# Soft MoE weights split in the cross-attention stage, and mu moved in 256 KB pieces in the routed experts

## The reference

```python
x = x + tanh(g_xattn[0]) * L0_xattn(ctx, ctx, layernorm(x), ssm_kernel, D, 8)     # long convolution
x = x + tanh(g_ffn[0])   * L0_ffn(layernorm(x), ...)      # shared expert + 8 routed experts, top 2
x = x + tanh(g_xattn[1]) * L1_xattn(layernorm(x), ctx, ...)   # linear attention
x = x + tanh(g_ffn[1])   * L1_ffn(x, gamma, beta, mu, scale, W1, b1, W2, b2)

def L1_ffn(...):                       # Soft MoE: 16 experts x 128 slots
    x_ln = layernorm(x) * gamma + beta
    logits = einsum('bnd,des->bnes', l2norm(x_ln) * scale, l2norm(mu, axis=0))
    dispatch = softmax(logits, axis=1)            # over the tokens
    combine = softmax(logits.reshape(B, N, E * S), axis=-1)
    slot_in = einsum('bnd,bnes->besd', x_ln, dispatch)
    h = gelu(einsum('besd,edh->besh', slot_in, W1) + b1)
    slot_out = einsum('besh,ehd->besd', h, W2) + b2
    return einsum('bsd,bns->bnd', slot_out, combine)
```

## Time and profile before

| | |
|---|---|
| time, 3 runs | 1918.27, 1921.96, 1922.52 us; median 1921.96 |
| the profiled execution | time 1921.54 us, span 1919.8 us |
| PE busy | 1594.0 us (83%) |
| DVE busy | 1134.1 us (59%) |
| ACT busy | 735.5 us (38%) |
| POOL busy | 480.1 us (25%) |
| granted PE clock, mean | 0.939 of full speed |

### The profile page before, as it was taken

How to read it: one execution, slowest core, us unless ns; L and a number is a source line. 1 busy time by engine, 2 the same in 40 slices (tenths; PEclk the granted TensorE clock), 3 DMA queues, 4 the chain that set the end, 5 groups by cost and what they waited for, 6 DMA issues and landing times. The chain is left out here.

```text
span 1919.8 us, 27754 instructions
## 1 busy us (share of the span) xinstructions
PE 1594.0 (83%) x9596; PEld 927.9 (48%) x9596; DVE 1134.1 (59%) x2222; ACT 735.5 (38%) x1380; POOL 480.1 (25%) x368
## 2 busy tenths in 40 slices
PE   2978874899926988985879887586999999999997
PEld 2767762344413555552435444243555555555554
DVE  4978864555362222225768685566667676676664
ACT  2322112334321222213423332165656566565552
POOL 1334330444342433323232321134020110201000
PEclk9999996999967999996999999798999999999999
DMA  8323334333346555635330300643415143151432
GB/s 184 82 84 106 126 108 140 115 114 127 104 142 132 123 150 146 152 107 197 99 110 12 100 3 20 234 134 83 86 42 116 33 87 81 44 115 33 77 73 49
DMA packets 261179, 195.26 MB, mean 102 GB/s; under 512 B 183426, under 2 KB 212098, under 8 KB 259410
## 3 DMA queue, kind: packets, MB, share of 16 engines
q1 hardware_dynamic: 253920, 174.03, 33.6%
q0 software_dynamic: 5680, 18.62, 3.5%
q10 hardware_dynamic: 1474, 1.21, 0.3%
HBM read 110.37 MB, written 39.67 MB: 78 GB/s over the span
## 5 line engine op out<-in xcount | busy, mean ns | idle before, releaser
L1958 POOL TENSOR_TENSOR s_h_lo<-s_h,s_h_hi 128x512 f16<-128x512 f32 x32 | 37.0, 1155 | 515.9 <-DVE s_h_hi L2176 515.9
L1180 DVE TENSOR_TENSOR e_h<-e_up,e_silu 128x352 f32<-128x352 f32 x39 | 20.5, 525 | 177.7 <-ACT e_silu L1142 177.7
L507 PE MATMUL ring<-prod_hi,toep 128*128 128x288 f16 x320 | 92.8, 290 | 32.6 <-DVE terms L427 21.6
L2194 PE MATMUL s_ring<-w_mu,s_xt_hi 128*128 128x512 f16 x256 | 98.4, 384 | 15.1 <-DVE s_xt_lo L2095 14.7
L306 POOL TENSOR_TENSOR prod_lo<-prod,prod_hi 128x2304 f16<-128x2304 f32 x16 | 73.3, 4581 | 102.5 <-ACT prod_hi L343 97.8
L2195 PE MATMUL s_ring<-w_mu,s_xt_hi 128*128 128x512 f16 x256 | 98.1, 383 | 0.0
L2196 PE MATMUL s_ring<-w_mu,s_xt_lo 128*128 128x512 f16 x256 | 98.0, 383 | 0.0
L2100 DVE TENSOR_REDUCE s_top<-s_lg 128x1 f32<-128x512 f32 x64 | 43.9, 686 | 90.5 <-ACT s_lg L2004 90.3
L2194 PE MATMUL s_acc<-w_w_hi,s_g_hi 128*128 128x512 f16 x256 | 97.1, 379 | 0.2
L2194 PE MATMUL s_ring<-w_w,s_xt_hi 128*128 128x512 f16 x256 | 97.0, 379 | 0.0
L2195 PE MATMUL s_ring<-w_w,s_xt_hi 128*128 128x512 f16 x256 | 97.0, 379 | 0.0
(11 more groups left out here) (386 smaller groups left out, 4750.4 us busy)
## 6 DMA issues: line engine op xcount, KB each, us to landing
expert_rows<-e_y SPq DMA_DIRECT2D x39, 256.0 KB, 2.3
toep<-ssm_split SPq DMA_DIRECT2D x14, 512.0 KB, 5.8
stage<-in_L_ffn_gate_w SPq DMA_DIRECT2D x8, 704.0 KB
stage<-in_L_ffn_up_w SPq DMA_DIRECT2D x8, 704.0 KB
c_rows<-in_ctx SPq DMA_DIRECT2D x8, 512.0 KB, 10.2
x_rows<-in_x SPq DMA_DIRECT2D x8, 512.0 KB
res<-in_x SPq DMA_DIRECT2D x128, 32.0 KB
w_in<-in_L_ffn_W SPq DMA_DIRECT2D x16, 256.0 KB, 5.2
```

Source lines behind the costliest of these rows:

```text
L507: nc.tensor.matmul(out, w_hi, hi, start=(n == 0), stop=False)
L2194: mm(out_, a[0], b_[0], start=first, stop=False)
```

## The change

Four edits that belong together:

1. The convolution no longer touches W1: 16 loads, 16 stores, 16 ACT copies and 16 POOL subtractions go.
2. `xattn_phase` gets an operation P, 32 times: 16 pieces of W1 and 16 of W2, 256 KB each. ACT copies a piece to its high half, and ACT itself issues the store of the piece before it and the load of the piece after next; POOL subtracts. P stands behind each QF and behind every second AT.
3. In the Soft MoE the operation Q goes. W2 comes ready from `w2_split` in four DMAs of 1 MB, behind W1 and b1. In the first batch the last four E/T pairs move from ahead of X to behind the first gelu (`body0`).
4. In the routed experts mu moves in 16 pieces of 256 KB, loaded at tiles 1 to 8 and then each behind a store, one for each tile; the arithmetic's places shift, and SP stores the result of tile n-5 behind the transpose of tile n, not that of n-3.

The core of the diff:

```diff
@@ xattn_phase
+        parts = iter(range(PARTS))
+        schedule = [o for at in schedule for o in ([at, (0, "P", next(parts))] if at[1] == "QF" or at[1] == "AT" and at[2] % 2 else [at])]
+            def load_part(n):
+                v = n % PART_BUFS
+                if n < NJ * KD:
+                    act.dma_start(part_in[:, v, :].rearrange("p (e h) -> p e h", e=JE), w1_d[n // KD, n % KD]).then_inc(part_loaded[v], 16)
+                else:
+                    act.dma_start(part_in[:, v, :], w2[n - NJ * KD]).then_inc(part_loaded[v], 16)
+
+            def store_part(n):
+                m = n % (NJ * KD)
+                dst = (w1_out if n < NJ * KD else w2_out)[m // KD, m % KD]
+                act.wait_ge(part_hi, n + 1)
+                act.wait_ge(part_lo, n + 1)
+                act.dma_start(dst, part_q[:, n % PART_BUFS]).then_inc(part_stored[n % PART_BUFS], 16)
...
+                if op == "P":
+                    v = n % PART_BUFS
+                    act.wait_ge(part_loaded[v], (n // PART_BUFS + 1) * 16)
+                    if n >= PART_BUFS:
+                        act.wait_ge(part_stored[v], n // PART_BUFS * 16)
+                    A(part_q[:, v, 0, :], part_in[:, v, :], ACT.Copy).then_inc(part_hi, 1)
+                    if n >= 1:
+                        store_part(n - 1)
+                    if n >= 1 and n + 2 < PARTS:
+                        load_part(n + 2)
@@ expert_phase, SP
-            def load_mu(j):
-                if j >= 2:
-                    sp.wait_ge(MU["hi"], (j - 1) * KD)
-                    sp.wait_ge(MU["lo"], (j - 1) * KD)
-                sp.dma_start(mu_in[:, j % 2], mu_d[:, :, j * D:(j + 1) * D]).then_inc(mu_loaded[j % 2], 16)
+            def load_mu(j, c):
+                sp.dma_start(mu_in[:, j % 2, c, :], mu_d[:, c, j * D:(j + 1) * D]).then_inc(mu_loaded[j % 2], 16)
+            def store_mu(j, c):
+                sp.wait_ge(MU["hi"], j * KD + c + 1)
+                sp.wait_ge(MU["lo"], j * KD + c + 1)
+                sp.dma_start(mu_out[j, c], mu_q[:, :, c, :]).then_inc(MU["stored"], 16)
+            def background(n):
+                if 1 <= n <= 2 * KD:
+                    load_mu(*divmod(n - 1, KD))
+                for j, c in ((quarter_at(n, 13 + c), c) for c in range(KD)):
+                    if j is not None:
+                        store_mu(j, c)
+                        if j + 2 < NJ:
+                            load_mu(j + 2, c)
-                if n >= 3:
-                    store(n - 3)
-                if n < 2:
-                    load_mu(n)
-                if n >= SPAN + 3 and (n - 3) % SPAN == 0:
-                    j = (n - 3) // SPAN - 1
-                    store_mu(j)
-                    if j + 2 < NJ:
-                        load_mu(j + 2)
+                if n >= LAG:
+                    store(n - LAG)
+                background(n)
@@ soft_moe_phase
-                  + softmax_in(2) + w2_split(0, 2) + E(0) + late("Z", 4) + softmax_in(3) + w2_split(2, 4) + E(1) + late("Z", 5) + softmax_in(4)
-                  + w2_split(4, 6) + E(2) + late("Z", 6) + softmax_in(5) + w2_split(6, 8) + late("Z", 7) + softmax_in(6) + softmax_in(7) + softmax_in(8)
-                  + w2_split(8, 10) + softmax_in(9) + E(3) + w2_split(10, 12) + softmax_in(10) + E(4) + w2_split(12, 14) + E(5) + w2_split(14, 16)
-                  + E(6) + E(7))
+                  + softmax_in(2) + E(0) + late("Z", 4) + softmax_in(3) + E(1) + late("Z", 5) + softmax_in(4)
+                  + E(2) + late("Z", 6) + softmax_in(5) + E(3) + late("Z", 7) + softmax_in(6) + softmax_in(7) + softmax_in(8) + softmax_in(9) + softmax_in(10))
+        for op in body:
+            body0 += [op]
+            if op == (0, "HG", 0):
+                body0 += E0(4) + E0(5) + E0(6) + E0(7)
+            for j in range(NJ):
+                sp.dma_start(w.w2[:, j].rearrange("p q e d -> p (q e d)"), w2_split[j]).then_inc(w2_in[j], 16)
```

More of the change, by code:

```diff
@@ L270, in _ @@
                     load_toeplitz(s + T_BUFS)
-                if s == 0:
-                    for v in range(W1_BUFS):
-                        load_w1(v)
                 store(s)
@@ L368, in _ @@
                     split(s + 2)
-                split_w1(s)
         @block.vector
@@ L1068, in _ @@
                                              ).then_inc(gathered[n % U], 16)
-                if n >= U and n - U < NJ * SPAN:
-                    quarter(*divmod(n - U, SPAN))
+                background(n)
+            for n in range(TILES, FIRST + PERIOD * (NJ - 1) + 16):
+                background(n)
         @block.tensor
@@ L1115, in step, with background @@
                     last.then_inc(contracted, 1)
-            def quarter(j, part):
-                if part == 2:
+            def background(n):
+                j = quarter_at(n, 4)
+                if j is not None:
                     pe.wait_ge(MU["ones"], 1)
@@ L1124, in quarter @@
                     last.then_inc(MU["summed"], 1)
-                if part == 4:
+                j = quarter_at(n, 6)
+                if j is not None:
                     pe.wait_ge(MU["inverted"], j + 1)
@@ L1163, in quarter @@
                     nc.scalar.activation(mu_scale[:, :], mu_ps[:, :], ACT.Copy).then_inc(MU["scale"], 1)
-                if part in (6, 7):
-                    if part == 6:
-                        act.wait_ge(MU["stored"], j * 16)
-                    for c in range((part - 6) * 2, (part - 6) * 2 + 2):
+                for j, c in ((quarter_at(n, 9 + c // 2), c) for c in range(KD)):
+                    if j is not None:
+                        if not c:
+                            act.wait_ge(MU["stored"], j * KD * 16)
                         act.wait_ge(MU["scaled"], j * KD + c + 1)
                         nc.scalar.activation(mu_q[:, 0, c, :], mu_in[:, j % 2, c, :], ACT.Copy).then_inc(MU["hi"], 1)
-            over_tiles(step, quarter)
+            over_tiles(step, background)
         @block.vector
@@ L1193, in step, with background @@
                     nc.vector.tensor_copy(y[:, u, :], out_ps[:, b, :]).then_inc(y_done, 1)
-            def quarter(j, part):
-                if part == 3:
+            def background(n):
+                j = quarter_at(n, 5)
+                if j is not None:
                     inv = mu_inv[:, j, :]
@@ L1489, in _ @@
             act.wait_ge(bg_negated, 1)
+            for n in range(PART_BUFS):
+                load_part(n)
             run(step)
+            store_part(PARTS - 1)
+            for u in range(PART_BUFS):
+                act.wait_ge(part_stored[u], -(-(PARTS - u) // PART_BUFS) * 16)
         @block.vector
@@ L2273, in step @@
                         at = n % 2 * N + t * P
-                        last_ = three(acc[:, t, :], [a[:, n // 2 % G_BUFS, at:at + P] for a in g], [a[:, n, :] for a in w.w2],
+                        last_ = three(acc[:, t, :], [a[:, n // 2 % G_BUFS, at:at + P] for a in g], [w.w2[:, n // JE, q, n % JE, :] for q in range(2)],
                                       False, n == EXPERTS2 - 1)
```

170 lines of the change are left out of this document (65 added, 105 removed).

## The result

The changed kernel takes 1872.8 us (median of 4 runs, 1869.8 to 1875.1), the one before, beside it, 1920.1 (1915.1 to 1922.5): a ratio of 0.976, 95% interval 0.973 to 0.978. The profiled execution takes 1872.76 us, with a span of 1870.8; PE is busy for 1594.3 us, as long as before.

A forecast was written before the change was run, and what follows sets the result against it. Bounds: W1's stores ending the convolution, late expert transposes, a DVE-ACT ring in attention, PE's wait for X in Soft MoE. From 1921.5 us, -7 - 24 + 12 - 8 = -27 gave 1894 us, range 1878 to 1909.

The forecast's parts named there:

- The convolution, -7 forecast: Convolution without W1: 5 us at the stage's end plus 2 us from POOL's subtractions; bounds 3 to 9.
- My 0 for ACT's wait: Convolution: ACT's waits for W1 loads vanish, but gain 0, since prod_hi behind them is needed a step later.
- the lower of my two bounds (3.2): Convolution's end: next stage's first load 5.0 to 3.2 us sooner without W1's last stores; 5 taken.
- the lock on POOL's port: Convolution: POOL's W1 subtractions block DVE on a shared port; 1 us at one place, 1 for the others.
- The routed experts, -24 forecast: Routed experts: smaller mu pieces and later stores remove 22.6 us of transpose waits and 4 of slow clock, less 2 to 3.
- my 4 for the clock: Routed experts: PE runs slowly after the two long waits; removing them gains 2 us each.
- The linear attention, +12 forecast: Linear attention: operation P costs 9.5 us over three chunks, 1.5 at the start, 1 at context loads; bounds 0 to 25.
- Neither has room: Linear attention, Q cycle of 5.61 us: DVE and PE are both full, and ACT's next work is what DVE waits for.
- the ring: Linear attention: DVE and ACT wait on each other in the Q cycle; P lengthens it from 5.61 to 6.9 us.
- The Soft MoE, -8 forecast: First Soft MoE batch: X 13.4 us earlier, 6.4 given back behind the gelu less 2.1 of waiting; 8 taken, bounds 4 to 11.
- issues cost nothing, all else at its best: Linear attention: ACT's DMA issues stay off the path, 0 to +3; about 1885 us, or 1876 at best; chance 0.20.
- The slower rival: Linear attention: every P puts its full 1.7 us on the path, 54 us in all; about 1940 us; chance 0.06.

The follow-up runs named there:

- the nine kernels of the table: Versions of the kernel before or the changed one whose convolution carries all of W1's loads and stores, in varied order or queue; 1881.1 to 1920.8 us.
- with the tile early and W1 as before: Kernel before, all W1 work kept, each Toeplitz tile issued ahead of the residual loads and W1's transfers; 1920.8 us.
- with W1's traffic on ACT's queue and the tile early: Kernel before, W1's transfers issued by ACT, Toeplitz tiles ahead of residual loads: 1910.1 us; changed kernel with such traffic and order, no W1 arithmetic: 1885.6 us.
- the kernel with the lag alone: Kernel before, routed experts storing tile n-5's result behind the transpose of tile n, not n-3's; mu still in 1 MB transfers; 1901.3 us.

## Why the prediction was right and wrong

**The convolution, -7 forecast, -19.5 measured: the step that failed** is "ACT's waits for W1 loads go as well, but the prod_hi behind them is needed a step later: 0", and with it that W1's transfers had no price in the steps. I read only the last wait at two places, the end and POOL. PE's wait of 1.8 to 3.1 us at the start of each step, named in part as DVE's, stood in the profile, and its length belonged to a DMA. W1 was a third of the stage's bytes (0.52 of 1.57 MB a step). Its transfers alone, with no copy and no subtraction, took the step from 11.3 back to 13.4 us. In eight of the nine kernels of the table that have all of them PE's wait ends 0.1 us after the tile has landed, whether W1's issues stand ahead of it, behind it or on another queue; in the ninth, with the tile early and W1 as before, it is W1's own load and `prod_hi` behind it. The step is 13 to 14 us on average each time. My 0 for ACT's wait was right only as long as the tile was as late. The end gave 3.1 us and not 5, the lower of my two bounds (3.2). For the lock on POOL's port I had 2 us: with W1's traffic on ACT's queue and the tile early the stage is 288.0 us long with all the copies and subtractions and 286.9 without. These 1.1 us are less than the spread of the stage, so no run shows this term.

**The routed experts, -24 forecast, -27.7 measured, or -23.7 by the means.** The mechanism and its size held: every wait behind the first tile went, 22.6 us, and PE's busy time fell from 237.6 to 229.0 us, as matmuls at the 1.2 GHz level went with them. The 2 to 3 us that I left for remaining waits were not there, and my 4 for the clock were somewhat low. But the 22.6 us of waits were those of one execution; five more kernels with that code had 15.5 to 19.3, so 27.7 is the upper end of what the change gives. I had not said which of the two edits does it: it is the lag, for some 20 of them.

**The linear attention, +12 forecast, +5.7 measured: the term was mis-sized.** The place was right: the cycles that hold TC and CB in three chunks, nothing in AT (pitch of `a_a_hi` 4.24 and 3.77 us as before) and nothing in the last chunk (cycles of 5.18 us as before). I took a copy and two issues as 1.7 us one behind the other. The issues run beside ACT's own activations, and the copy fits into ACT's wait: a cycle with P grew by 0.4 to 1.0 us, not by 1.3. "Neither has room" was wrong for ACT: its waits of 1.65 and 0.35 us were room for the copy. I had this as a rival (0.20) with the right objection that only 0.35 us of it is in the ring; that DVE's share of the ring took the rest is argued, not measured. The first cycle of a chunk was covered in two chunks, as I had it (7.4 us before and after), but not in the third: 7.4 us against 5.9, where PE waited 4.05 us for the context and not 2.42.

**The Soft MoE, -8 forecast, -7.8 measured.** X came 15.2 us earlier (75.3 us from the stage's start, not 90.5) against 13.4, the eviction L0 9.3 (9.1 forecast). PE's wait at G is 6.45 us, just over my 2 to 6.

The rivals: the time lies near that of "issues cost nothing, all else at its best" (1876), but the attention did cost 5.7; most of the 22 us between forecast and measurement are the convolution (12.5), then the attention (6.3) and the experts (3.7). The slower rival's condition, 1.2 us for each P, was far off: 5.7 / 32 = 0.18.

**Still open:** why the small transfers and the large ones don't overlap in the convolution, even from two queues, and whether fewer and larger transfers of the result and the residual would give the 9 to 10 us at 50 GB/s back; neither was tried. Nor was it followed what sets a single step under this load: the same traffic made the stage 285.9 to 302.4 us long (the longest in the kernel with the lag alone, whose convolution is that of before), with steps from 11.3 to 18.2 us.

## What to carry to other kernels

When work leaves a stage, price its transfers too: find the rate at which the large ones move in that stage, and ask whether they run beside the small ones or in turn with them. An average over many steps can't tell: 120 GB/s looked like a ceiling here and was a mean of 50 and 250. Where they go in turn, as here, moving issues about or to another queue does not help, and taking bytes away does. A wait that ends last hides others of nearly its length, and its named releaser may not be the last: look up when each thing waited for was there. And when two edits hit one wait, try each alone, and compare with the spread of that stage in other kernels before giving either the credit: here the lag gave some 20 us, and the 4.2 that the size of the transfers seemed to give alone is within the spread.

## What the runs showed of the hardware

DMA issues on ACT's queue overlap its activations: from `a_q_hi` to exp it was 0.98 us before, 1.06 with the copy, and 1.38 with the copy and issues of 0.53 and 0.63 us. Beside large transfers the issues of small ones stretch: eight 32 KB loads took 7.95 us at 180.96 us in the kernel with W1 on ACT's queue and the tile early, and 5.2 in the kernel before. Transfers of 32 KB issued one after the other moved 50 GB/s, and tile and W1 some 250 GB/s, in the same steps. A DVE product of 128 x 2048 from SBUF took 5.21 us in place of 2.28 beside POOL's subtraction. The Trainium skill, "SBUF — State Buffer", section "SBUF: two separate sides", has the port pair of the two as an exclusive lock for a whole instruction; the row agrees, since 179.72 + 2.28 = 182.0 and the product ends at 181.87.
